# A fourth of the shared expert's gate and up products moved into the last steps of the cross-attention, and GpSimd's table entries moved ahead of the delta's factor

## What is computed

```python
x = x + self_attention(layernorm(x))
x = x + cross_attention(layernorm(x), ctx)      # delta: scaled, normalised, gamma, beta
f = layernorm(x)
logits = f @ gate.T; scores = softmax(logits)   # 3 of 8 groups, then 6 of 64 experts a token
# each expert takes its first 192 tokens: silu(f Wg.T) * (f Wu.T) @ Wd.T
shared = silu(f @ Sg.T) * (f @ Su.T) @ Sd.T     # width 704, for all tokens
out = x + routed + shared
```

## Time and profile before

| | us |
|---|---|
| median of the runs | 1599.75 |
| the profiled execution | 1597.56 |
| its span | 1595.9 |
| cross-attention ends, experts start (first transfer of weights) | 655.8 |
| shared stage's first product | 1376.8 |
| busy: TensorE / VectorE / ScalarE / GpSimd | 1486.6 / 1139.3 / 897.5 / 772.4 |

### The profile page before, as it was taken

The page is one execution under the profiler, slowest core; times in us unless marked ns, Lnnn a source line. Parts: engine busy times, 40 slices in busy tenths (PEclk is TensorE's granted clock), DMA queues, the critical chain, the costliest instruction groups (busy, mean ns, idle before and its releaser), DMA issues.

```text
span 1595.9 us, 30498 instructions
## 1 busy us (share of the span) xinstructions
PE 1486.6 (93%) x10360; PEld 1232.2 (77%) x10360; DVE 1139.3 (71%) x2054; ACT 897.5 (56%) x1769; POOL 772.4 (48%) x957
## 2 busy tenths in 40 slices
PE   6999998999999865499999999999999999999997
PEld 4788886778888754388888888888888888777866
DVE  5677757557888787577777777777777777565656
ACT  4565666644544331187777777777777778412111
POOL 2122234233365556265565555565555564437543
PEclk9999999999999976599999999999999999999999
DMA  6012212222211110598777787777887775437553
GB/s 205 7 55 85 62 54 91 95 71 74 75 66 41 41 54 34 202 365 294 270 266 259 275 289 264 267 267 263 277 289 263 268 262 200 137 119 225 178 177 119
DMA packets 109217, 275.48 MB, mean 173 GB/s; under 512 B 16592, under 2 KB 16592, under 8 KB 109136
## 3 DMA queue, kind: packets, MB, share of 16 engines
q1 hardware_dynamic: 91392, 223.53, 41.0%
q0 software_dynamic: 15360, 50.34, 9.8%
q10 hardware_dynamic: 2384, 0.53, 0.2%
HBM read 232.41 MB, written 41.94 MB: 172 GB/s over the span
## 4 chain that ended last, share of the span: by engine, by line
PE 55%; DVE 2%; DMA 1%; issue 0%; POOL 0%; ACT 0%; SPq 0%; DVEq 0%; POOLq 0%
PE e_gu L2386 18%; PE e_gu L2388 9%; PE e_dn_rest L2414 5%; PE e_tr L49 3%; PE e_dn_main L41 3%; PE e_dn_main L43 3%; PE e_dn_main L42 3%; PE h_gt L41 1%; PE h_gt L43 1%; PE h_gt L42 1%; PE h_up L43 1%; PE h_up L41 1%; PE h_up L42 1%; PE h_dn L41 1%; DVE h_acc L2663 1%; PE h_dn L42 1%
## 5 line engine op out<-in xcount | busy, mean ns | idle before, releaser
L2149 POOL TENSOR_TENSOR e_hid<-e_h_raw,e_hid 128x128 fp32r<-128x128 f32 (+1 forms) x192 | 165.6, 863 | 221.3 <-ACT e_hid L2214 221.3
L2386 PE MATMUL e_gu<-e_xT_hi_lo,e_wg 128*128 128x384 f32 (+1 forms) x768 | 231.5, 357 | 1.6 <-issue 1.6
L2386 PE MATMUL e_gu<-e_xT_hi_lo,e_wu 128*128 128x384 f32 (+1 forms) x768 | 230.4, 355 | 0.0
L2388 PE MATMUL e_gu<-e_xT_hi_lo,e_wu 128*128 128x192 f32 (+1 forms) x768 | 193.3, 252 | 0.0
L2388 PE MATMUL e_gu<-e_xT_hi_lo,e_wg 128*128 128x192 f32 (+1 forms) x768 | 193.1, 251 | 0.0
L2157 POOL TENSOR_TENSOR e_wd<-e_raw_d,e_wd 96x512 fp32r<-96x512 f32 x64 | 131.6, 2056 | 35.8 <-ACT e_wd L2199 35.8
L2386 PEld LDWEIGHTS e_gu<-e_xT_hi_lo,e_wg 128*128 128x128 f32 (+1 forms) x768 | 138.0, 180 | 6.8 <-issue 2.6
L2292 DVE TENSOR_TENSOR e_total<-e_gu,e_low 128x384 f32<-128x384 f32 (+1 forms) x192 | 105.5, 549 | 51.5 <-ACT e_low L2209 51.5
L2388 PEld LDWEIGHTS e_gu<-e_xT_hi_lo,e_wg 128*128 128x128 f32 (+1 forms) x768 | 139.8, 182 | 1.4
L2386 PEld LDWEIGHTS e_gu<-e_xT_hi_lo,e_wu 128*128 128x128 f32 (+1 forms) x768 | 137.9, 180 | 3.8
L2388 PEld LDWEIGHTS e_gu<-e_xT_hi_lo,e_wu 128*128 128x128 f32 (+1 forms) x768 | 139.7, 182 | 0.0
(11 more groups left out here) (341 smaller groups left out, 4049.3 us busy)
## 6 DMA issues: line engine op xcount, KB each, us to landing
e_raw_g<-in_L_ffn_Wg_dram SPq DMA_DIRECT2D x64, 704.0 KB, 4.3
e_raw_u<-in_L_ffn_Wu_dram SPq DMA_DIRECT2D x64, 704.0 KB, 5.7
e_raw_d<-in_L_ffn_Wd_dram SPq DMA_DIRECT2D x64, 512.0 KB, 5.9
y_dram<-e_y_main SPq DMA_DIRECT2D x64, 256.0 KB, 6.2
e_raw_d<-in_L_ffn_Wd_dram SPq DMA_DIRECT2D x64, 192.0 KB, 6.4
y_dram<-e_y_rest SPq DMA_DIRECT2D x64, 128.0 KB, 7.0
s_xr<-in_x_dram SPq DMA_DIRECT2D x16, 256.0 KB, 3.8
x_dram<-s_x SPq DMA_DIRECT2D x16, 256.0 KB, 2.5
```

The costliest lines, as they stand in the source:

```text
L2149: pool.tensor_tensor(hid[b][1][0:n, c, :], h_raw[g.odd][b][0:n, c, 0:P], hid[b][0][0:n, c, :].bitcast(F32), ALU.subtract).then_inc(s_hl, 1)
L2386: pe.matmul(bank[0:n, 0:2 * CAP], w[b][0][:, k, m:m + n], xT[:, :, k, toks], start=k == 0, stop=False)
L2388: ins = pe.matmul(bank[0:n, 0:CAP], w[b][1][:, k, m:m + n], xT[:, 0, k, toks], start=False, stop=k == KC - 1)
```

## The change

The gate and up products of quad 2 (tiles 8 to 11) are made in the cross-attention, from the transposed rows that `logits` makes anyway (now kept for these tiles, `final_T`). The 12 weight pieces are loaded in steps 11 and 12 (512-byte runs), split by ScalarE and GpSimd at the ends of steps 12 to 15, and multiplied by TensorE as units 0, 1 (step 14), 2, 3 (step 15) and 4 to 10 (tail). ScalarE evicts them (Silu for a gate unit), GpSimd multiplies gate and up, and SyncE stores the hidden rows in DRAM. On GpSimd the entries of a step come ahead of `delta_factor`. In the feed-forward, the shared stage takes quads 0, 1, 3 and then 2, whose `hidden` is gone: its rows are loaded and only split. The loops over quads are written out, the transposes of the next quad come between the steps of `hidden` into a second pair of buffers, x3 has four accumulators, and VectorE's order is new. Buffers of the cross-attention that are no longer read are laid over by the new ones.

```diff
+SHARED_SPLITS = {12: range(0, 3), 13: range(3, 7), 14: range(7, 9), 15: range(9, 11)}
@@ cross_phase, SyncE, in the loop over t, after store_xf(t - 2)
+                if t == 11:
+                    sp.wait_ge(s_pj, filled(("q", QUADS - 1, KC - 1)))
+                    load_shared(range(0, FIRST_LOADS))
+                if t == 12:
+                    load_shared(range(FIRST_LOADS, INNER))
+            for c in range(SCN):
+                sp.wait_ge(s_fm, c + 1)
...
+                sp.dma_start(shared["hidden"][c * P + rows.start:(c + 1) * P, :], f_hid[c][rows, :]).then_inc(s_fst, 16)
@@ GpSimd
-                if t >= 1:
-                    delta_factor(t - 1)
                 for g in range(NG - 3):
...
                             table_entries(g, i)
+                if t >= 1:
+                    delta_factor(t - 1)
+                for i in SHARED_SPLITS.get(t, ()):
+                    shared_lo(i)
...
             for i in range(PAIR):
                 table_entries(NG - 3, i)
+            for c in range(SCN):
+                shared_hidden(c)
@@ ScalarE
+            def shared_hi(i):
+                if i < FIRST_LOADS:
+                    act.wait_ge(s_fw[0], 16 * FIRST_LOADS)
...
                 exps(t, 0)
+                if t == 14:
+                    shared_out(0)
...
                     attn_hi(t - 1)
+                if t == 14:
+                    shared_out(1)
                 if t >= 2:
                     final_norm(t - 2)
+                if t == 15:
+                    shared_out(2)
...
                 exps(t, 1)
+                if t == 15:
+                    shared_out(3)
...
+                for i in SHARED_SPLITS.get(t, ()):
+                    shared_hi(i)
             rinv_out(BATCH - 1)
             attn_hi(BATCH - 1)
+            shared_out(4)
             final_norm(BATCH - 2)
             final_hi(BATCH - 2)
+            shared_out(5)
             route_exp(BATCH - 2)
             final_norm(BATCH - 1)
+            shared_out(6)
             final_hi(BATCH - 1)
+            shared_out(7)
             route_exp(BATCH - 1)
+            for i in range(8, INNER):
+                shared_out(i)
@@ TensorE
                 scores(t)
+                if t == 14:
+                    shared_unit(0)
                 if t >= 1:
                     widen(t - 1)
+                if t == 14:
+                    shared_unit(1)
...
+                if t == 15:
+                    shared_unit(2)
+                    shared_unit(3)
                 if t >= 2:
                     turn_final(t - 2)
...
+            shared_unit(4)
             widen(BATCH - 1)
             positions(BATCH, one)
             table_part(BATCH, one - 1)
             turn_final(BATCH - 2)
             project_out(BATCH - 1)
+            shared_unit(5)
             logits(BATCH - 2)
+            shared_unit(6)
             turn_final(BATCH - 1)
+            shared_unit(7)
             logits(BATCH - 1)
+            shared_unit(8)
             positions(BATCH, two)
+            shared_unit(9)
             table_part(BATCH, one)
             table_part(BATCH, two)
+            shared_unit(10)
             positions(BATCH, three)
@@ shared_programs, SyncE
+        for n in range(4):
+            load_x3(n)
+        for stored in free["y_stored"]:
+            sp.wait_ge(*stored)
+        for c in range(SCN):
+            rows = slice(0, P) if c < FULL else slice(HALF, P)
+            sp.dma_start(raw_hid[rows, c, :], ahead_hidden[c * P + rows.start:(c + 1) * P, :]).then_inc(s_rh, 16)
+        for p in range(turns):
+            if p + 2 < turns:
+                sp.wait_ge(s_t, QT * (p + 1))
+                load_xf(sp, p + 1)
@@ VectorE, chunks(p, between): the six steps of a turn, with routed additions between them
+                if c:
+                    hidden_lo(p, c - 1)
+                if c in between:
+                    n, part = between[c]
+                    routed(n, range(3 * part, 3 * part + 3))
+            hidden_lo(p, FULL)
...
+        chunks(0, {3: (0, 0), 4: (0, 1)})
+        routed(1)
+        finish(0)
+        routed(2)
...
+        chunks(1, {1: (4, 0), 2: (4, 1), 3: (5, 0), 4: (5, 1), 5: (6, 0)})
...
+        chunks(2, {0: (8, 0), 1: (8, 1), 2: (9, 0), 3: (9, 1), 4: (10, 0), 5: (10, 1)})
+        finish(8)
+        for c in range(3):
+            hidden_lo(3, c)
+        routed(11)
+        finish(9)
+        for c in range(3, SCN):
+            hidden_lo(3, c)
+        finish(10)
+        routed(12)
+        finish(11)
+        routed(13)
+        finish(12)
+        routed(14)
+        finish(13)
+        routed(15)
+        finish(14)
+        finish(15)
@@ TensorE, in hidden(p), after the products of step c
+                if c in (2, 3) and p + 2 < turns:
+                    turn_tokens(pe, p + 1, 2 * (c - 2), 2 * (c - 1))
```

More of the change, by code:

```diff
@@ L2458, in shared_buffers, with shared_programs @@
                 carry=[sb(f"carry{b}", [P, 1]) for b in range(2)])
-def shared_programs(nc, sems, mine, own, raw, loaded, xf, x3, y_in, out, weight, slot, ident, experts):
-    quads = BATCH // QT
+def shared_programs(nc, sems, mine, own, raw, loaded, xf, x3, y_in, out, weight, slot, ident, experts, ahead_hidden):
+    order = [q for q in range(BATCH // QT) if q != AHEAD] + [AHEAD]
+    turns = len(order)
+    late = ExitStack()
     with ExitStack() as ctx:
@@ L2509, in shared_programs @@
         s_dn = sem("down_in_psum")
-        s_x3 = two(sem, "x3_loaded")
+        s_x3 = [sem(f"x3_loaded{b}") for b in range(4)]
+        s_rh = sem("raw_hidden_loaded")
         s_idx = two(sem, "idx_ready")
@@ new lines, in gpsimd, with gather @@
+    def gpsimd(pool):
+        pool.memset(ones[:], 1.0).then_inc(s_ones, 1)
+        pool.wait_ge(s_ones, 1)
+        def gather(n):
+            b = n % 2
+            if n >= 2:
+                pool.wait_ge(s_acc[b], TOPK * (n // 2))
+            pool.tensor_copy(idx[b][:], slot[:, tile(n) * TOPK:(tile(n) + 1) * TOPK]).then_inc(s_idx[b], 1)
+            pool.wait_ge(s_idx[b], n // 2 + 1)
+            for k in range(TOPK):
+                pool.indirect_dma_start(out=yk[b][:, k * H:(k + 1) * H], out_offset=None, in_=y_in,
+                                        in_offset=bass.IndirectOffsetOnAxis(ap=idx[b][:, k:k + 1], axis=0)
+                                        ).then_inc(s_yk[b][k], 16)
+        for stored in free["y_stored"]:
+            pool.wait_ge(*stored)
+        for n in range(BATCH):
+            gather(n)
@@ new lines, in scalar, with hidden_hi, turn @@
+    def scalar(act):
+        def hidden_hi(p, c):
+            late = p == turns - 1
+            if late:
+                src = raw_hid[:, c, :]
+            else:
+                act.wait_ge(s_mul, SCN * p + c + 1)
+                src = h_raw[c % 2][:]
+            if c < FULL:
+                act.activation(hid[late][0][:, c, :], src, ACT.Copy).then_inc(s_hh, 1)
+            else:
+                act.activation(hid_half[late][high_rows, :], src[high_rows, :], ACT.Copy).then_inc(s_hh, 1)
+        def turn(p):
+            for c in range(SCN):
+                if c in (3, 4) and p + 2 < turns:
+                    x_hi(act, p + 1, 2 * (c - 3), 2 * (c - 2))
+                act.wait_ge(s_gu, SCN * p + c + 1)
+                if c < FULL:
+                    act.activation(act_g[c % 2][:], gt[c % 2][:], ACT.Silu).then_inc(s_silu, 1)
+                else:
+                    act.activation(act_g[c % 2][high_rows, :], gt[c % 2][low_rows, :], ACT.Silu).then_inc(s_silu, 1)
+                if c:
+                    hidden_hi(p, c - 1)
+            hidden_hi(p, FULL)
+        split_hi(act, INNER, len(pieces))
+        act.activation(sd[1][low_rows, FULL, :], raw_d[low_rows, FULL, :], ACT.Copy).then_inc(s_wh, 1)
+        for p in range(turns - 1):
+            turn(p)
+        act.wait_ge(s_rh, 16 * SCN)
+        for c in range(SCN):
+            hidden_hi(turns - 1, c)
```

503 lines of the change are left out of this document (277 added, 226 removed).

## The result

The changed kernel takes 1605.91 us, the median of 17 runs (1602.08 to 1613.30), beside 1600.68 (1597.22 to 1605.90, 17 runs) for the kernel before in the same session. The ratio is 1.0039, 95% interval 1.0028 to 1.0050. The forecast was 1577.8 us, 1562 to 1592: wrong in size and in sign. The profiled execution of the changed kernel took 1612.85 us (span 1611.2), near the top of its runs.

What follows compares the result with a forecast made beforehand. TensorE was taken to bound the shared expert's stage, busy 201.7 of 220 us, with idle time at the cross-attention's end. 27.3 us saved less 5.3 lost gave 22.0: 1599.75 - 22.0 = 1577.8 us, range 1562 to 1592.

Steps and rivals of the forecast that it cites:

- Entries ahead of the factor: Cross-attention steps 4 to 9: GpSimd's table entries delay VectorE by 11.5 us; 2 us taken as cost, bounds 0 and 11.5.
- A: Stretch from ScalarE's copy of the spread inverse sums in step 1 to that in step 12; forecast 200.2 us, before 198.2.
- GpSimd's added work: Cross-attention's end: the added products of hidden rows and six stores fit in before GpSimd's last twelve entries end the phase.
- the cross part: Whole cross-attention: 3.3 + 2.0 = 5.3 us lost, with bounds of 3 gained and 17 lost.
- B: Stretch from step 12's copy of the spread inverse sums to the start of the experts; forecast 116.7 us, before 113.4.
- The shared stage: Shared expert's stage, 1376 to 1596 us: shorter by 27.3 us, with GpSimd's gathers carrying the end.
- The first wait for token rows: Shared stage, first hidden turn: TensorE waits 5.5 us for rows queued on SyncE, bounds 0 and 10.
- D: Stretch from the first matmul of `h_gt` to the last output `h_o`; forecast 187.6 us, before 214.9.
- that case: Last four tiles of the shared stage: gathers at 9.4 us each instead of 8.7 make the forecast 2.1 later.
- ScalarE's table loads: Cross-attention's last steps: nine Silu/Exp switches of 1.28 us, four on the path; 3.3 us late with the other additions there.
- The rival by the drain of the Trainium skill: Cross-attention: every switch costs 2.66 us, some 12.4 more, 1590.2 us; 5 of the 14 in a hundred given to ScalarE's chain.
- Late weights: Cross-attention, end of step 12: ScalarE waits for five weight loads; 1604.5 us if they land at 582.7; chance 0.04.

## Why the prediction was wrong

**Entries ahead of the factor, taken at 2.0 us: the first step that failed.** The five delays were read right: 2.7 + 1.6 + 3.4 + 2.5 + 1.3 = 11.5 on VectorE, and A grew by 11.4. I discounted them because TensorE was busy 49.3 of 50 us with a unit queued in front of the first wait. But a full TensorE means that what is lost can't be made up later, not that it has work in reserve. Step by step the distances grew by what VectorE was late, and TensorE was busy 4.2 us less in 450 to 500 alone. The right reading of the bounds 0 and 11.5 was the upper one. Measured: 9.8 us of median when it is taken back up to step 11, and 9.6 when the order alone is put into the kernel before.

**GpSimd's added work, priced at nothing: the second.** "The added products of hidden rows and their six stores fit in before that end" asked only whether GpSimd has the time. It has; yet VectorE stands still beside it. 5.2 us for the products and 6.3 for the low parts, none of it in the sum or its bounds: the cross part lost 28.1 us (A and B) where 5.3 was the forecast and 17 the bound. The prediction asked of every engine what is queued behind it, but not what its operations do to the engine beside it. The kernel before had a row for it that I passed over: VectorE's low part of the attention took 1.25 us at 615.21, in place of some 0.7, beside a two-tensor operation of GpSimd (614.64 to 615.91).

**The shared stage, 27.3 forecast, 16.8 in the trace: right in mechanism, one term missing.** The first wait for token rows was sized at 5.5 and measured 5.8; the low parts' stalls at 5.2 and measured 4.2. TensorE's hidden products in turn 2 took 30.1 (1528.5 to 1558.6) for 29.9. Missing was the same transfer one turn later, behind the stores in SyncE's queue: turn 1's hidden products ran from 1468.5 to 1506.9, 38.4 us for the 31.7 forecast. Against the forecast the parts of D are over by 1.5 (hidden, turn 0), 1.2 (its down), 6.7, 0.2 (down, turn 1), 0.2 (hidden, turn 2) and 0.8 (the rest), 10.6 in all. The last gathers went at 9.2 to 9.5 us a tile (starts at 1574.02, 1583.25, 1592.71) for the 8.7 taken; the prediction had named that case. Loading rows first gave 7.4 of median back.

**ScalarE's table loads, 3.3 for all of steps 12 to the end: right.** Nine loads of 1.28, no gap behind them but the two waits for VectorE, and 3.9 us when they go. The rival by the drain of the Trainium skill ("ScalarE: Activation LUTs", What ACT_TABLE_LOAD costs) fell. I had priced it at 12.4 with all nine switches, though I had traced only four on the path (5.5). The whole of B missed by 13.4, though, and mainly by the causes above: A and B are 4.7 and 4.4 shorter in the two traces without products or low parts, and the rows show 5.0 and 6.0 of stretched operations. The eleventh unit stood 1.1 us ahead of the last positions.

**Late weights: fell.** ScalarE's first split followed the route's Exp without a wait, and each transfer landed in 4.2 us (median). Their q unit was itself 16.8 us late, at 555.68, and it still sufficed.

**The chance of slower, 0.04.** One sign that I had named came: the phase ended over 10 us late. But my only slower rival was a transfer. Four terms of the kind "covered" (2.0 for 11.4, and nothing for 5.2, for 6.3 and for turn 1's 6.7) added up against one saving that was known exactly. The likelier slower rival was that two or three covers fail together.

The terms close the sum: 9.4 (A) + 13.4 (B) - 2.5 (C) + 10.5 (D) + 5.3 ahead of step 1 is 36.1 of the 37.3 us by which this execution's span is over the forecast for it (1611.2 against 1573.9). The median is over by 28.1, since the execution was a slow one of its kernel. What makes the stretch ahead of step 1 vary, and with it some of the kernel's spread of 11 us, isn't settled. Nor is what the new order gains from step 12 on, or what of B no experiment accounts for.

## What to carry to other kernels

Where a row shows an engine busy 49.3 of 50 us, as here, count a delay of its feeder in full, unless another row shows the idle that absorbs it. When work is moved to GpSimd, ask not whether it has time but which operations of VectorE on two SBUF tensors run then, and put the work beside waits or reads of PSUM: `c_attn`, which multiplies a PSUM operand by an SBUF one, took 0.68 us at 598.76 and at 618.33 with GpSimd's two-tensor residual beside it (598.94, 618.50), and 0.68 or 0.69 in every step. When a loop over stages is written out, walk down SyncE's queue for each turn, not only for the first: a load behind a store is as late as the engine that the store waits for.

## What the runs showed of the hardware

A small operation can be shut out far beyond one instruction. VectorE's 64 x 2 addition, due at 667.67, ended at 672.82, when GpSimd's fifth product in a row was over at 672.80; it was let in at none of the boundaries between them. In the other case, at 612.88, the two engines took turns: 1.76 and 1.66 us on VectorE, and 1.74 for GpSimd's second subtraction, where 1.28 was the first one's.

Not every operation of GpSimd does it. Its table entries read one tensor and two columns of scalars, and beside them VectorE's one-hot rows on two tensors took 1.01 us for two (at 659.45, entries from 653.92 to 666.70), as without them; beside a subtraction they took 2.12. So by these traces the form of GpSimd's operation matters as well. The entries are of two-byte numbers and the subtractions of four-byte ones, and no run separates that from the count of tensors.
